# A preLN layer in fp32 halves on one core: VectorE's step begins elsewhere, q in four passes, fewer warming transposes, two loop rounds

## The reference

```python
# attention without softmax, in batches of 1024 rows
n1 = layernorm(x);  Q, K, V = n1 @ wq.T, n1 @ wk.T, n1 @ wv.T        # D = 64
energy = einsum('bnd,bne->bde', K, V)
x = x + (Q @ energy) * sqrt(3/64) @ wo.T
# feed-forward, then five steps of an integrate-and-fire neuron
n2 = layernorm(x);  y = square(relu(n2 @ W_fc.T)) @ W_proj.T         # 256 -> 1024 -> 256
for _ in range(5): reset = mem > 1; mem = 0.9*mem + y - reset; count += mem > 1
x = x + count / 5
```

## Time and profile before

| | |
|---|---|
| median of 3 runs | 505.34 us (504.41 to 507.06) |
| the profiled execution: time | 501.43 us |
| the profiled execution: span | 499.5 us |
| mean granted TensorE clock in it | 0.993 |
| busy: PE / DVE / ACT / POOL | 478.6 / 342.4 / 286.4 / 237.3 us |

### The profile page before, as it was taken

The page is one execution under the profiler, slowest core; times in us unless marked ns, Lnnn a source line. Parts: engine busy times, 40 slices in busy tenths (PEclk is TensorE's granted clock), DMA queues, the critical chain, the costliest instruction groups (busy, mean ns, idle before and its releaser), DMA issues.

```text
span 499.5 us, 9518 instructions
## 1 busy us (share of the span) xinstructions
PE 478.6 (96%) x3080; PEld 432.7 (87%) x3080; DVE 342.4 (69%) x966; ACT 286.4 (57%) x519; POOL 237.3 (48%) x196
## 2 busy tenths in 40 slices
PE   7899899999999979999999997999999999999995
PEld 6698689899889869898898996898898999999995
DVE  4457658777676776767677855768867674939447
ACT  3427666657566655666566564665746664656540
POOL 1444664473736526374544634545363743535340
PEclk9999999999999999999999998999999999999998
DMA  8413021130403113040312212131110101010102
GB/s 310 99 44 69 17 42 44 54 75 36 93 0 85 43 55 73 0 126 0 85 42 64 63 43 42 43 79 47 55 30 0 42 2 42 1 43 1 44 1 84
DMA packets 60705, 26.46 MB, mean 53 GB/s; under 512 B 55552, under 2 KB 56192, under 8 KB 60416
## 3 DMA queue, kind: packets, MB, share of 16 engines
q1 hardware_dynamic: 60672, 26.09, 19.1%
HBM read 17.69 MB, written 8.39 MB: 52 GB/s over the span
## 4 chain that ended last, share of the span: by engine, by line
PE 79%; DVE 10%; issue 6%; ACT 2%; DMA 1%; POOL 1%; SPq 0%; DVEq 0%; POOLq 0%
PE hid_ps L814 10%; PE hid_ps L815 10%; PE hid_ps L816 10%; PE y_ps L816 10%; PE y_ps L815 10%; PE y_ps L814 10%; PE work_ps L856 3%; PE y_ps L823 2%; DVE stat L592 2%; PE work_ps L922 2%; DVE cnt L701 2%; PE work_ps L923 2%; DVE cnt L720 1%; PE kv_ps L814 1%; PE kv_ps L815 1%
## 5 line engine op out<-in xcount | busy, mean ns | idle before, releaser
L355 POOL TENSOR_TENSOR hid_l<-hid,hid_h 128x512 fp32r<-128x512 f32 x128 | 165.2, 1296 | 204.7 <-ACT hid_h L409 204.5
L398 ACT ACTIVATE relu<-hid_ps 128x512 f32<-128x512 f32 x128 | 76.6, 598 | 112.1 <-PE hid_ps L816 110.6
L815 PE MATMUL y_ps<-wdn_l,hid_h 128*128 128x256 f32 x480 | 136.1, 284 | 0.0
L816 PE MATMUL y_ps<-wdn_h,hid_l 128*128 128x256 f32 x480 | 136.1, 283 | 0.0
L814 PE MATMUL y_ps<-wdn_h,hid_h 128*128 128x256 f32 x480 | 135.7, 283 | 0.0
L814 PE MATMUL hid_ps<-x2T_h,wup_h 128*128 128x512 f32 x256 | 105.5, 412 | 0.5 <-ACT relu L398 0.3
L815 PE MATMUL hid_ps<-x2T_l,wup_h 128*128 128x512 f32 x256 | 100.9, 394 | 0.0
L816 PE MATMUL hid_ps<-x2T_h,wup_l 128*128 128x512 f32 x256 | 100.3, 392 | 0.0
L814 PEld LDWEIGHTS y_ps<-wdn_h,hid_h 128*128 128x128 f32 x480 | 92.0, 192 | 5.1
L815 PEld LDWEIGHTS y_ps<-wdn_l,hid_h 128*128 128x128 f32 x480 | 92.0, 192 | 4.9
L816 PEld LDWEIGHTS y_ps<-wdn_h,hid_l 128*128 128x128 f32 x480 | 91.9, 192 | 0.0
(11 more groups left out here) (125 smaller groups left out, 611.7 us busy)
## 6 DMA issues: line engine op xcount, KB each, us to landing
xs<-x_dram SPq DMA_DIRECT2D x15, 512.0 KB, 3.3
out_dram<-x SPq DMA_DIRECT2D x15, 512.0 KB, 2.7
x_block<-x_dram SPq DMA_DIRECT2D x104, 64.0 KB, 2.5
hid<-w_up_dram SPq DMA_DIRECT2D x1, 1024.0 KB, 8.1
x<-w_down_dram SPq DMA_DIRECT2D x1, 1024.0 KB, 10.2
xs<-x_dram SPq DMA_DIRECT2D x2, 256.0 KB, 2.8
out_dram<-x SPq DMA_DIRECT2D x1, 256.0 KB, 2.0
out_dram<-x SPq DMA_DIRECT2D x2, 128.0 KB, 1.9
```

Of the source, the lines that this page charges most:

```text
L355: nc.gpsimd.tensor_tensor(hid_l[:, i % 2, c, :], hid[:, c % 4, :], hid_h[:, i % 2, c, :].bitcast(f32), ALU.subtract).then_inc(hid_ready, 1)
L398: nc.scalar.activation(relu[:, c % 2, :], hid_ps[c % 2][:, :], ACT.Relu).then_inc(relu_done, 1)
L815: mm(dst, a[0], b[1], start=False, stop=False)
L816: return mm(dst, a[1], b[0], start=False, stop=stop)
```

## The change

Four things are done.

1. VectorE's step. The second pair's 12 operations of group i-2 stand at the start of step i (they stood at the end of step i-1), in two halves of six. Between the halves stand `turn_blocks`, `q_low_half` and `energy_sum`; after them `eo_low_half`, then `first_moments`. On GpSimd the reciprocal deviation of group i+3 moves from c = 1 to c = 4.
2. q. The weights of q hold, side by side, 64 high and 64 low columns (`wq_hl`). Two passes of all 128 columns take x's high half, two of 64 columns x's low half. The products with the low weights now lie in PSUM partitions 64 to 127 and have to be added: `q_low_half` is two operations, by way of `kv_scaled`, with a semaphore between them, and `kv_scale` waits for it.
3. The lead-in. The rounds of `keep_warm` go from 8, 4, 2, 16, 4 to 3, 2, 2, 12, 4; ScalarE's and VectorE's lead-in lists are in another order.
4. FIRST is 2: steps 0 and 1, and 10 to 16, are written out, and the loop has two rounds (steps 2 to 5 and 6 to 9).

```diff
-FIRST = 1
+FIRST = 2
 LOOPS = (GROUPS - 3 - FIRST) // UNROLL
@@ GpSimd, step
-                    if c == 1 and there(r, i + 3):
+                    if c == (1 if is_first(r, i) else 4) and there(r, i + 3):
                         inverse_deviation(r, 2 if is_first(r, i) else i + 3, 0)
@@ ScalarE, q_high_half
-                nc.scalar.activation(qT[:, n % 2, :], q_bank(r, n)[:, :], ACT.Copy).then_inc(q_high, 1)
+                nc.scalar.activation(qT[0:HEAD, n % 2, :], q_bank(r, n)[0:HEAD, :], ACT.Copy).then_inc(q_high, 1)
@@ VectorE, kv_scale
+                if not isinstance(r, int) or n >= 2:
+                    dve.wait_ge(q_ready, 3 if isinstance(r, int) and n == 2 else upto(r, n))
@@ VectorE, q_low_half
-                nc.vector.tensor_tensor(qT[HEAD:P, n % 2, :], q_bank(r, n)[HEAD:P, :],
-                                        as_f32(qT[HEAD:P, n % 2, :]), ALU.subtract).then_inc(q_ready, 1)
+                dve.wait_ge(kv_ready, 2 if isinstance(r, int) and n < 3 else upto(r, n + 1))
+                if there(r, n - 1):
+                    dve.wait_ge(q_ready, upto(r, n))
+                nc.vector.tensor_tensor(kv_scaled[HEAD:P, :], q_bank(r, n)[0:HEAD, :],
+                                        as_f32(qT[0:HEAD, n % 2, :]), ALU.subtract).then_inc(q_rest, 1)
+                dve.wait_ge(q_rest, upto(r, n + 1))
+                nc.vector.tensor_tensor(qT[HEAD:P, n % 2, :], q_bank(r, n)[HEAD:P, :], kv_scaled[HEAD:P, :], ALU.add)\
+                    .then_inc(q_ready, 1)
@@ VectorE, step
+                if there(r, i - 2):
+                    spikes(r, i - 2, 1, range(0, PAIR_OPS // 2))
                 if there(r, i + 3):
                     turn_blocks(r, i + 3)
-                    first_moments(r, i + 3)
...
                     energy_sum(r, i + 2)
+                if there(r, i - 2):
+                    spikes(r, i - 2, 1, range(PAIR_OPS // 2, PAIR_OPS))
                 if there(r, i + 2) and closes_batch(i + 2):
                     eo_low_half(r, i + 2)
+                if there(r, i + 3):
+                    first_moments(r, i + 3)
...
-                if there(r, i - 1):
-                    spikes(r, i - 1, 1, range(PAIR_OPS))
@@ TensorE, project_q
+                both = [wq_hl[:, k, :, :].rearrange("p s d -> p (s d)") for k in range(EC)]
+                mm(q_bank(r, n)[:, :], both[0], xT_h[:, n % 2, 0, :], start=True, stop=False)
                 for k in range(EC):
-                    last = three(q_bank(r, n)[:, :], (wqq_h[:, k, :], wqq_l[:, k, :]),
-                                 (xT_h[:, n % 2, k, :], xT_l[:, n % 2, k, :]), k == 0, k == EC - 1)
+                    mm(q_bank(r, n)[0:HEAD, :], wq_hl[:, k, 0, :], xT_l[:, n % 2, k, :], start=False, stop=False)
+                last = mm(q_bank(r, n)[:, :], both[1], xT_h[:, n % 2, 1, :], start=False, stop=True)
@@ TensorE, lead-in
-            keep_warm(8)
+            keep_warm(3)
...
-            keep_warm(4)
+            keep_warm(2)
             energy_times_wo(0, PER_BATCH - 1)
             keep_warm(2)
             attend(0, 0)
-            keep_warm(16)
+            keep_warm(12)
```

More of the change, by code:

```diff
@@ L91, in build @@
         wkv_h, wkv_l = (sb(f"wkv_{s}", [P, EC, 2 * HEAD], f32r) for s in "hl")
-        wqq_h, wqq_l = (sb(f"wqq_{s}", [P, EC, 2 * HEAD], f32r) for s in "hl")
+        wq_hl = sb("wq_hl", [P, EC, 2, HEAD], f32r)
         wup_h, wup_l = (sb(f"wup_{s}", [P, EC, HID], f32r) for s in "hl")
@@ L174, in build @@
         averager_ready, mean_done = sem("averager_ready"), sem("mean_done")
-        wkv_centred, wqq_centred = sem("wkv_centred"), sem("wqq_centred")
+        wkv_centred, wq_centred = sem("wkv_centred"), sem("wq_centred")
         wkv_high, wkv_ready = sem("wkv_high"), sem("wkv_ready")
-        wqq_high, wqq_ready = sem("wqq_high"), sem("wqq_ready")
+        wq_high, wq_ready = sem("wq_high"), sem("wq_ready")
         wup_high, wup_ready = sem("wup_high"), sem("wup_ready")
@@ L188, in build @@
         kv_turned, kv_in_scale, kv_high, kv_ready = sem("kv_turned"), sem("kv_in_scale"), sem("kv_high"), sem("kv_ready")
-        q_done, q_high, q_ready = sem("q_done"), sem("q_high"), sem("q_ready")
+        q_done, q_high, q_rest, q_ready = sem("q_done"), sem("q_high"), sem("q_rest"), sem("q_ready")
         energy_done, energy_out, energy_ready = sem("energy_done"), sem("energy_out"), sem("energy_ready")
@@ L519, in _ @@
             high_half_of_weights(wkv_centred, wkv_raw[:, :], wkv_h, wkv_high)
-            high_half_of_weights(wqq_centred, wqq_raw[:, :], wqq_h, wqq_high)
+            act.wait_ge(wq_centred, 1)
+            nc.scalar.activation(wq_hl[:, :, 0, :], wqq_raw.rearrange("p (k s n) -> p k s n", k=EC, s=2)[:, :, 0, :], ACT.Copy).then_inc(wq_high, 1)
             xT_high_half(0, 0)
             xT_high_half(0, 1)
+            half_of_columns(w_loaded["up"], wup_raw, wup_h, wup_high, 0)
             kvT_out(0, 0)
+            q_high_half(0, 0)
+            half_of_columns(w_loaded["up"], wup_raw, wup_h, wup_high, 1)
+            kvT_out(0, 1)
             kv_high_half(0, 0)
-            half_of_columns(w_loaded["up"], wup_raw, wup_h, wup_high, 0)
-            q_high_half(0, 0)
-            kvT_out(0, 1)
+            q_high_half(0, 1)
             kv_high_half(0, 1)
-            half_of_columns(w_loaded["up"], wup_raw, wup_h, wup_high, 1)
+            half_of_columns(w_loaded["down"], wdn_raw, wdn_h, wdn_high, 0)
             energy_first_half(0, PER_BATCH - 1)
-            q_high_half(0, 1)
+            half_of_columns(w_loaded["down"], wdn_raw, wdn_h, wdn_high, 1)
             eo_high_half(0, PER_BATCH - 1)
-            half_of_columns(w_loaded["down"], wdn_raw, wdn_h, wdn_high, 0)
-            half_of_columns(w_loaded["down"], wdn_raw, wdn_h, wdn_high, 1)
             x2T_high_half(0, 0)
@@ L780, in step @@
                     kv_low_half(r, i + 3)
-                if there(r, i - 1):
-                    spikes(r, i - 1, 1, range(PAIR_OPS))
             centre_weights(w_loaded["kv"], wkv_raw[:, :], 0, wkv_centred)
-            centre_weights(w_loaded["qq"], wqq_raw[:, :], 1, wqq_centred)
+            centre_weights(w_loaded["qq"], wqq_raw[:, :], 1, wq_centred)
             first_moments(0, 0)
@@ L789, in _ @@
             xT_low_half(0, 0)
-            low_half_of_weights(wqq_high, wqq_raw[:, :], wqq_h, wqq_l, wqq_ready)
+            dve.wait_ge(wq_high, 1)
+            nc.vector.tensor_tensor(wq_hl[:, :, 1, :], wqq_raw.rearrange("p (k s n) -> p k s n", k=EC, s=2)[:, :, 0, :], as_f32(wq_hl[:, :, 0, :]),
+                                    ALU.subtract).then_inc(wq_ready, 1)
+            xT_low_half(0, 1)
             first_moments(0, 1)
-            xT_low_half(0, 1)
             kv_scale(0, 0)
             kv_low_half(0, 0)
-            q_low_half(0, 0)
             kv_scale(0, 1)
             kv_low_half(0, 1)
+            q_low_half(0, 0)
             energy_sum(0, PER_BATCH - 1)
@@ L884, in project_q @@
                     pe.wait_ge(xT_ready, n + 1)
-                    pe.wait_ge(wqq_ready, 1)
+                    pe.wait_ge(wq_ready, 1)
                 else:
                     pe.wait_ge(x2T_ready, upto(r, n - 1))
+                both = [wq_hl[:, k, :, :].rearrange("p s d -> p (s d)") for k in range(EC)]
+                mm(q_bank(r, n)[:, :], both[0], xT_h[:, n % 2, 0, :], start=True, stop=False)
                 for k in range(EC):
-                    last = three(q_bank(r, n)[:, :], (wqq_h[:, k, :], wqq_l[:, k, :]),
-                                 (xT_h[:, n % 2, k, :], xT_l[:, n % 2, k, :]), k == 0, k == EC - 1)
+                    mm(q_bank(r, n)[0:HEAD, :], wq_hl[:, k, 0, :], xT_l[:, n % 2, k, :], start=False, stop=False)
+                last = mm(q_bank(r, n)[:, :], both[1], xT_h[:, n % 2, 1, :], start=False, stop=True)
                 last.then_inc(q_done, 1)
```

## The result

484.03 us median (483.65 to 486.42, 4 runs) against 504.99 for the kernel before (504.41 to 507.06, 4 runs): ratio 0.9588 [0.9546, 0.9629], 21 us faster, and 0.4 us from the forecast of 483.6. The profiled execution took 483.65 us, its span 481.6, against 501.4 and 499.5: 17.9 us less in the span, where 19.7 were forecast.

A forecast was written before the change was run, and what follows sets the result against it. TensorE, busy 478.6 of 499.5 us, was taken as the bound. Waits 10.3, q 6.0 and lead-in 3.4 make 19.7 off 501.4, giving 481.7; the middle between that and 485.6 is 483.6, range 478 to 490.

The forecast's parts named there:

- The waits (10.3): Odd steps: TensorE's waits for VectorE's energy sum and the clock fall in step 9 all go, 10.3 us.
- 2.2 us in hand: Odd steps without the issue stall: the energy sum would be ready 2.2 us before TensorE asks for it.
- q (6.0): q's projection: two fewer TensorE passes, 0.46 us per group, in groups 3 to 15, 6.0 us gained.
- Rival A: q's narrow passes: each change of width drains TensorE, 1.0 us gained in place of 6.0, time 488.6; chance 0.12.
- Going round, counted 0: Loop's going-round ahead of step 6: VectorE's 2.5 us stall may come again but is covered, cost 0.
- Lead-in and step 0 (3.4): Before step 1: 2.1 + 1.0 + 0.8 - 0.5 = 3.4 us gained, bounds 2 and 4.5.
- The 2.1 for the projections: Lead-in: with 12 first transposes in place of 32, the projections start 2.1 us earlier.
- the new list puts that copy first: Lead-in: ScalarE's copy ahead of weight copies, and shorter q, let group 1's k and v turn about 1.0 us earlier.
- The excess of the timed runs (3.9, halved): Timed median 3.9 us above the profiled execution, cause unknown; forecast takes the middle of 481.7 and 485.6.
- B: Odd steps: a new 1 us wait at attend or the energy product, 489.6; or going-round at step 6, 487.6; chance 0.10.
- D: Energy sum still last because ScalarE's half is late; the 10.3 us loss stays, time 494; chance 0.03.
- C: Lead-in: clock falls with fewer transposes and stays low through steps 0 and 1, 5 us slower, 510; chance 0.03.

The follow-up runs named there:

- first2_alone: Kernel before the change with only FIRST = 2 in place of 1, so two loop rounds; median 496.36 us, ratio 0.9856.
- old_order: Changed kernel with VectorE's step and GpSimd's power put back in the order of before; median 496.80 us, ratio 0.9858.
- lead: Changed kernel, lead-in: GpSimd's low weight halves held until both groups' k and v are done, ScalarE's high half of k and v earlier; 482.00 us, ratio 0.9568.
- before: The kernel before the change, unedited, timed beside the others; median 504.99 us beside the changed kernel.

## Why the prediction was right, and where it was off

The forecast was 483.6 and the time is 484.03; its parts, from the profiled executions (step 1 begins at its first up pass, at 59.13 before and 57.30 after; the others at a turning of k and v):

| stretch | forecast gain | measured |
|---|---|---|
| lead-in and step 0 | 3.4 | 1.83 |
| step 1 | 0.48 + 0.46 | 0.96 |
| steps 2 to 12 | 9.82 + 11 x 0.46 = 14.9 | 14.63 |
| step 13 to the end | 0.46 | 0.48 |
| sum | 19.7 | 17.9 |

*The waits (10.3).* Right, step by step: step 3 gave 1.10 (0.63 + 0.46), step 5 3.70 (3.22 + 0.46), step 9 5.19 (4.71 + 0.46). `first2_alone` and `old_order` show both causes apart: 6.6 us went with the stalls ahead of steps 5 and 9, the rest needs the new order. Of the 2.2 us in hand 2.0 are there. What is last for the sum now is ScalarE's half, and the list ahead of it could not be shortened to any use.

*q (6.0).* Right: 5.7 by the run with six passes. Rival A falls with the 0.23 us starts: no drain shows around the passes of 64 columns. So either they are no change of mode in the sense of the page of the Trainium skill that the prediction names, or its rule does not hold for them.

*Going round, counted 0.* Mis-sized by 0.36 us. The forecast took the stall for the price of every going-round; `first2_alone` shows one without. The cover assumed (3.3 us for q's low half) held, since `attend` never waits; but the stall ran on through the list to the normalisation at the end of step 6, which the forecast did not look at (218.06 in the trace, and the turning behind it took 1.30 for 1.03). It varied, 2.1 to 3.2 us in the eight profiles of kernels with the new order, four q passes and a going-round, and step 6 with it, 27.7 to 28.8.

*Lead-in and step 0 (3.4).* The term that was mis-sized: 1.83, 2.18 in the lead-in less 0.35 in step 0. The 2.1 for the projections came, and 0.8 for the last transposes is in reach of the rows (turning at 32.12, waiting 0.44 for the normalisation, none for transposes). What failed is "the new list puts that copy first ... about 1.0": the copy of k and v did come first, TensorE turned group 1 at 16.12 instead of 19.91, and then waited 1.19 and 2.11 us for L580, which ScalarE fed 1.85 late and GpSimd's weight halves held up. Behind the gap of 2.11 the clock fell for 3.4 us as well. The durations were taken from a profile in which nothing of GpSimd's lay beside that operation; moved, it met the weight halves. With both taken away (`lead`) the span is 480.1, close to the 479.8 of the forecast: 1.5 us, of which 0.2 is a shorter step 6. Step 0 lost 0.35 (forecast 0.5), and its normalisation beside GpSimd takes 3.39 us as it took 3.43 before: a loss in both kernels that the forecast's rows showed and I did not read.

*The excess of the timed runs (3.9, halved).* It went nearly whole: 484.03 - 483.65 is 0.4. So the gain in the profiled execution was 1.8 too large in the forecast and that of the excess 1.6 too small, and they cancelled; the closeness of 483.6 is partly luck. The runs of before point to the clock: of those with a mean clock of 0.993 five of six have spans of 498.4 to 499.9, those at 0.980 to 0.983 (eight) 502.8 to 504.5. The slower ones spent more time at the lower level; where was not recorded, so that it stood behind the waits for the energy sum is likely and not shown.

*Rivals.* B came only as the 0.36 above, behind the going-round; D is touched (0.21 us of ScalarE ahead of the sum) and costs nothing; C was the right place, the lead-in, and a small part of the price.

## What to carry to other kernels

Find the wait that TensorE pays, read the list that the awaited engine works through ahead of it, and move out what nobody awaits; the gain was forecast to 0.1 us per step from rows alone. A duration read from a trace holds only with the neighbours it had there: before an operation is moved, look at what GpSimd does beside it at its new time. And measure parts of a change together as well as apart: without the new order the q and lead-in edits together gave nothing (496.80 against 496.36), and two edits that showed nothing in the time alone took 2.5 us off step 0 combined. A run that removes a cause should also be read where the cause is still there: `first2_alone` was right in its time and wrong about the going-round.

## What the runs showed of the hardware

- A VectorE operation on two operands in SBUF that meets a GpSimd operation ends 0.4 to 0.55 us after that one: 0.69 became 1.25, 1.31 and 2.69. One with an operand in PSUM (L570) kept its 0.69 beside the same GpSimd work. Four normalising operations (1.38 us alone) and two of GpSimd's (2.5 us alone) took 3.39 together.
- TensorE's clock fell to 1.2 GHz in the lead-in of the changed kernel and of all eleven made from it, and not in `before` and `first2_alone`, though a wait of 1.77 us stands there too. It stayed low for 3.4 us in the seven profiles in which it fell up to 2.0 us behind a wait (1.6 to 2.1 us), for 6.8 in four in which it fell during one, and for 20 with no transposes, where TensorE stood idle again and again.
- VectorE stalled for 2.1 to 3.3 us in issue at each going-round of the loop, except the one of `first2_alone`, where it didn't stall. TensorE lost 0 to 1.3 us by it at step 6, and 2.6 and 4.1 us (the second with a fall of the clock) at steps 5 and 9 before.
- A pass of 64 weight columns starts 0.23 us behind the one before, as one of 128 does.
